# Four-layer decoder on one Trainium2 core: new instruction orders in the second self attention, the last cross attention and the last feed forward

## The chip, the cores and the metric

The kernel runs on one core of one Trainium2 chip. A core has TensorE (PE in the profile: matmuls and transposes, results in PSUM), VectorE (DVE), ScalarE (ACT), GpSimd (POOL) and the DMA queues, here issued by SyncE (SP). Each engine runs its own instruction list in order; they meet only at semaphores. The metric is the device time of one execution in microseconds, as the median of several runs.

## The reference, cut to what matters

The model is a pre-norm decoder of 4 layers over x of 32 × 128 × 128, float32: each layer adds a self attention, a cross attention to a context of 32 × 120 × 96, and a feed forward. Twelve blocks in all. The change touches three of them.

```python
# layer 1, self attention: 16 heads of 8; two inner gradient steps of a small linear model per head
Z = k @ W0;  y1, vjp1 = vjp(ln, Z);  dz1 = vjp1(y1 - v)
KK = tril(k @ k.T);  Z2 = Z - KK @ dz1;  y2, vjp2 = vjp(ln, Z2);  dz2 = vjp2(y2 - v)
ctx = q @ W0 - tril(q @ k.T) @ (dz1 + dz2)
ctx = (ctx - mean) * rsqrt(var + EPS)          # over positions and channels of a head
x = x + (ctx * gn_g + gn_b) @ Wout + bout

# layer 3, cross attention: 16 heads of 8
q = x_hat @ q_w + q_b;  k, v = split(cond @ kv_w + kv_b)
x = x + softmax(q * 8**-0.5 @ k.T) @ v @ proj_w + proj_b

# layer 3, feed forward: product keys, 4 heads, 64 + 64 keys, 8 x 8 candidates, best 8 of 512 experts
sx, sy = top_k(q @ keys, 8);  s, pk = top_k(sx[:, None] + sy[None], 8)
w = silu((x_hat @ down_embed[idx]) * softmax(s))
x = x + silu(x_hat @ W_up.T) @ W_down.T + sum(w * up_embed[idx])
```

## The kernel before, in words

Each block is one function, and the twelve run one after the other. x stays in SBUF for the whole kernel, with 128 positions on the partitions. Inside a block every engine walks the same software pipeline, `skewed(engine, depth, n, per)` (line 180): step t works on item t in role 0, on item t-1 in role 1, and so on to the block's depth. `for b, u in item(2)` reads "the item that is two steps old"; b is its number, u the buffer it uses. The first steps are written out, the rest is a loop with `per` steps in its body. In what order an engine takes the roles' pieces inside one step is written by hand, and this order is what the change is about. `after(engine, semaphore, count)` is a wait that is left out where the count isn't positive; `chain(...)` makes DVE wait for its own instruction before.

*Self attention of layer 1* (`l1_attn`, line 1046): 16 steps' worth of pairs of sequences, depth 3. Role 0: ACT normalises x into x̂ (1209), PE transposes it (1284), ACT copies the transpose (1214), PE projects it with bias products (`projected`, 1252 to 1257) into the two PSUM halves r of `p_s`, ACT copies the projections (1217, 1218 and 1227, 1228) and squares z (1230); DVE reduces the squares (1173), and `gradient` (1126) makes dz1 and the outer products `outer1` (1199). Role 1: PE's `states` (1246) multiplies them by the triangular matrix into `p_s`, DVE's `applied` (1139) reads it (1143, 1146), z2, its squares (1221, 1167), a second gradient and `outer2` (1188). Role 2: the same with `outer2`, then the mean over the sequence by a product with ones (1280), centring (1163, 1164), squares (1224, 1170). Role 3: scaling of the context (1152, 1153), its transposes (1294), ACT's copy (1233), output product (1300), the residual (1177) and the statistics for the next block. The two PSUM halves of `p_s` are shared by `states1`, `states2` and the projections, with DVE's or ACT's reading between each two.

*Cross attention of layer 3* (`l3_xattn`, line 2683): 32 items, depth 4. Role 1: transpose of x̂ (2808), k, v and q products (2829, 2831, 2832). k is spread by head over `kTm` (2752). Role 2: scores with queries on the partitions (2793), four matmuls on four groups of 32 rows into four PSUM banks `p_s`; DVE takes the maximum per head (2730), PE transposes it (2811) and computes the scores transposed (2815) into the same banks, adds the negated maxima (2819), and ACT takes the exponential over all four banks (2773). Role 3: product with the values (2800), ACT's copy (2767), transposes (2825), division by the sum (2746, 2747), transpose of the heads (2835), copy (2781). Role 4: output product (2804), residual (2741), statistics.

*Feed forward of layer 3* (`l3_ffn`, line 2844): 16 pairs, depth 3. Role 0: x̂, transposes (3034), q product (3040), key products (3054). Role 1: DVE picks the best keys of each half and the candidates (2890 to 2905), forms all sums (2913, two instructions of 2048 columns), and ACT takes their exponentials (`exps`, 2950 to 2952). Role 2: dot products (2996), dense up product (3026) with ACT's Silu into hT (2965), masks and weights on DVE (2919 to 2931), ACT's `silus` of r=0. Role 3: `silus` of r=1 (2942, 2943: a Silu and a small one with accumulation for each of 4 heads), DVE adds the rest (`added`, 2878 to 2882), PE sums and transposes the weights over heads (`heads`, 2998 to 3004), ACT's `turned` copies them (2946 to 2948), PE makes the dense and the chosen output (3009, 3011, 3016), ACT copies it to x (2990). A table load (1.28 us) stands before the first exponential and before the first Silu of a step.

## Time and profile before

| | |
|---|---|
| median of 3 runs | 4558.21 us (4552.51 to 4561.47) |
| profiled execution | 4545.59 us |
| its span, first to last instruction | 4543.5 us |
| PE, DVE, ACT, POOL busy | 75%, 62%, 40%, 15% of the span |
| mean granted TensorE clock | 0.817 |

The profile is of one execution. Its busy shares are means over twelve blocks with different limits, so they say little about a block; the rows below are taken from stretches inside the three edited blocks. In a row of a timeline, the first number is the start in microseconds from the span's start and the second the duration; a bracket at the end gives the idle time of the engine before the instruction and who ended it. In a table of windows the last but two numbers are the granted clock of TensorE as a share of 2.4 GHz.

### The profile page before, as it was taken

What the parts mean: (1) busy time and instruction counts of PE and PEld (TensorE: products, weight loads), DVE (VectorE), ACT (ScalarE), POOL (GpSimd) and SP (SyncE); (2) the same over time, 40 slices, a digit from 0 to 9 for tenths busy, and PEclk for the clock granted to TensorE, in tenths of its full rate; (3) what the DMA queues carried; (4) which work ended last, traced back from release to release, by engine and by line L of the source; (5) the groups of instructions that cost most, each with busy time, mean ns of one, the idle gap of its engine ahead of it and who ended that gap; (6) DMA issues with size and microseconds to landing.
All of it is one profiled execution on the core that took longest, in us unless ns stands there. A gap on an engine that the chain in (4) does not pass through costs nothing. (4 is left out here: it accounts for less than half of the span.)

```text
span 4543.5 us, 71024 instructions
## 1 busy us (share of the span) xinstructions
PE 3398.5 (75%) x22014; PEld 2441.9 (54%) x22015; DVE 2817.2 (62%) x8303; ACT 1806.9 (40%) x5212; POOL 678.4 (15%) x867
## 2 busy tenths in 40 slices
PE   3567289456654885765888868999889997876887
PEld 3445289122222563544556755666567775555776
DVE  6556622588785775265886443444457775657886
ACT  1446233111112663212775333222145553436776
POOL 0044523000001776201000110000000000000000
PEclk9789599566766665577777777999989999997888
DMA  4030176100004000523000000000000000000000
GB/s 112 1 160 0 40 235 196 47 0 0 0 0 149 3 0 1 149 65 81 7 0 0 1 10 1 9 9 9 0 19 0 0 0 4 0 0 15 1 0 19
DMA packets 111454, 152.52 MB, mean 34 GB/s; under 512 B 21594, under 2 KB 88216, under 8 KB 109718
## 3 DMA queue, kind: packets, MB, share of 16 engines
q1 hardware_dynamic: 99822, 142.12, 10.1%
q0 software_dynamic: 11520, 9.05, 0.7%
q8 instruction: 52, 0.85, 0.1%
q14 instruction: 60, 0.49, 0.0%
HBM read 107.45 MB, written 58.50 MB: 37 GB/s over the span
## 5 line engine op out<-in xcount | busy, mean ns | idle before, releaser
L1249 PE MATMUL l_attn_p_s<-l_attn_outer,l_attn_upper 128*128 128x512 f32 x256 | 181.9, 876 | 204.4 <-DVE l_attn_outer L1188 131.0
L95 POOL TENSOR_TENSOR rstd<-vareps,minus_half 128x32 f32<-128x32 f32 x11 | 59.8, 5439 | 1456.6 <-DVE vareps L86 1323.6
L398 ACT ACTIVATE l_ffn_sg<-l_ffn_p_g 112x512 f32<-112x512 f32 x192 | 114.7, 597 | 391.9 <-PE l_ffn_p_g L378 367.1
L409 DVE TENSOR_TENSOR l_ffn_h<-l_ffn_sg,l_ffn_p_u 112x512 f32<-112x512 f32 x192 | 131.9, 688 | 172.7 <-PE l_ffn_p_u L381 171.7
L1249 PEld LDWEIGHTS l_attn_p_s<-l_attn_outer,l_attn_upper 128*128 128x128 f32 x256 | 70.2, 288 | 305.2 <-issue 185.5
L381 PE MATMUL l_ffn_p_u<-l_ffn_f_xTall,l_ffn_wu 128*112 x384 | 198.8, 600 | 7.7 <-DVE l_ffn_h L409 7.7
L1408 POOL DMA_INDIRECT slots_in<-l_xattn_x,l_xattn_slot x192 | 190.0, 990 | 82.3 <-issue 50.1
L378 PE MATMUL l_ffn_p_g<-l_ffn_f_xTall,l_ffn_wg 128*112 x384 | 199.0, 600 | 0.9 <-DVE l_ffn_al L2440 0.9
L387 PEld LDWEIGHTS l_ffn_p_o<-l_ffn_wd,l_ffn_h 112*128 112x128 f32 x1536 | 176.6, 192 | 15.7 <-issue 15.7
L2604 ACT ACTIVATE l_attn_E<-l_attn_p_s,l_attn_nm 128x128 f32<-128x128 f32 x512 | 181.2, 386 | 2.8 <-DVE l_attn_nm L2562 2.7
L387 PE MATMUL l_ffn_p_o<-l_ffn_wd,l_ffn_h 112*128 112x128 f32 x1536 | 176.7, 275 | 0.0
L418 DVE SCALAR_TENSOR_TENSOR x<-l_ffn_p_o,l_ffn_cw,x 128x128 f32 x256 | 85.5, 351 | 112.6 <-PE l_ffn_p_o L387 112.6
L2621 PEld LDWEIGHTS l_attn_p_y<-l_attn_xT,l_attn_wqkv 128*128 128x128 f32 x1024 | 131.6, 194 | 34.1 <-issue 32.9
L2621 PE MATMUL l_attn_p_y<-l_attn_xT,l_attn_wqkv 128*128 128x128 f32 x1024 | 137.6, 278 | 1.5 <-DVE l_attn_qT L2566 1.5
L3004 PEld LDWEIGHTS l_ffn_p_w<-ident,l_ffn_w 128*128 128x128 f32 x1024 | 129.8, 207 | 9.4 <-DVE l_ffn_w L2882 5.2
L3004 PE MATMUL l_ffn_p_w<-ident,l_ffn_w 128*128 128x128 f32 x1024 | 130.3, 290 | 5.9 <-DVE l_ffn_w L2882 4.2
L381 PEld LDWEIGHTS l_ffn_p_u<-l_ffn_f_xTall,l_ffn_wu 128*112 128x112 f32 x384 | 68.7, 179 | 106.7 <-issue 98.2
L2604 ACT ACTIVATION_READ_ACCUMULATOR l_attn_E<-l_attn_p_s,l_attn_nm 128x1 f32 x512 | 115.6, 226 | 0.0
L378 PEld LDWEIGHTS l_ffn_p_g<-l_ffn_f_xTall,l_ffn_wg 128*112 128x112 f32 x384 | 66.6, 179 | 83.4 <-issue 82.8
L3040 PE MATMUL l_ffn_p_q<-l_ffn_xT,l_ffn_wq 128*128 128x256 f32 x128 | 55.6, 609 | 59.3 <-ACT l_ffn_xT L2968 59.3
L2562 DVE TENSOR_REDUCE l_attn_nm<-l_attn_p_s 128x8 f32<-128x1024 f32 x64 | 78.1, 1221 | 30.6 <-PE l_attn_p_s L2648 30.6
L2773 ACT ACTIVATE l_xattn_E<-l_xattn_p_s 120x2048 f32<-120x2048 f32 x32 | 60.1, 1878 | 91.3 <-PE l_xattn_p_s L2819 91.3
(785 smaller groups left out, 9545.8 us busy)
## 6 DMA issues: line engine op xcount, KB each, us to landing
l_experts_w<-in_L_ffn_w SPq DMA_DIRECT2D x72, 512.0 KB, 4.2
slots_in<-l_xattn_empty SPq DMA_DIRECT2D x8, 2145.0 KB, 24.0
shares_out<-l_xattn_zero SPq DMA_DIRECT2D x24, 512.0 KB, 11.3
l_combine_got<-shares_out SPq DMA_DIRECT2D x16, 768.0 KB, 4.4
l_attn_toep<-kernel_rows SPq DMA_DIRECT2D x1, 8192.0 KB, 31.8
xattn_toep<-ssm_rows SPq DMA_DIRECT2D x1, 8192.0 KB
l_slots_w<-in_L_ffn_w SPq DMA_DIRECT2D x32, 176.0 KB, 2.3
l_experts_x<-slots_in SPq DMA_DIRECT2D x72, 65.0 KB
```

The lines of the kernel that those rows point to most:

```text
L378: pe.matmul(X.p_g[0:X.FP, k % 2], X.wg[:, w, f * X.FP:(f + 1) * X.FP], x, start=True, stop=True).then_inc(s.gate_psum, 1)
L381: pe.matmul(X.p_u[0:X.FP, k % 2], X.wu[:, w, f * X.FP:(f + 1) * X.FP], x, start=True, stop=True).then_inc(s.up_psum, 1)
L387: mm = pe.matmul(X.p_o[:, v, q * P:(q + 1) * P], X.h[:, v, f, q * P:(q + 1) * P], X.wd[:, w, f * P:(f + 1) * P], start=(f == 0), stop=(f = ...
L398: act.activation(X.sg[:, k % 2], X.p_g[0:X.FP, k % 2], ACT.Silu).then_inc(s.silu_ready, 1)
L409: dve.tensor_tensor(X.h[:, k // X.FC, k % X.FC], X.sg[:, k % 2], X.p_u[0:X.FP, k % 2], ALU.mult).then_inc(s.h_ready, 1)
L418: add = dve.scalar_tensor_tensor(out=row(R.x, b), in0=X.p_o[:, v, q * P:(q + 1) * P], scalar=weight, in1=row(R.x, b), op0=ALU.mult, op1=AL ...
L1249: mm = pe.matmul(p_s[:, r, a], upper[:], outer[:, r, a * 512:(a + 1) * 512], start=True, stop=True)
L1408: pool.indirect_dma_start(xb, bass.IndirectOffsetOnAxis(ap=slot[:, b, k:k + 1], axis=0), x6[:, u, k], None, bounds_check=last, oob_is_err= ...
L2562: dve.tensor_reduce(nm[:, u % 2], p_s[:, u % 2].rearrange("p a (h t) -> p (a h) t", t=P), AX.X, ALU.max, negate=True).then_inc(s.max_ready, 1)
L2604: e = act.activation(E[:, u % 2, h], p_s[:, u % 2, odd, c * P:(c + 1) * P], ACT.Exp, bias=nm[:, u % 2, h:h + 1], accum_out=sums[:, u % 2, ...
L2621: mm = pe.matmul(p_y[:, c * P:(c + 1) * P], wqkv[:, w:w + P], xT[:, u // 2], start=True, stop=True)
L3004: mm = pe.matmul(p_w[:, c * P:(c + 1) * P], w[:, v, r, n:n + P], R.ident[:], start=(h == 0), stop=(h == H - 1))
```

## The change

Only orders inside a step change, with the semaphore counts that go with them, and three pieces are split in two. No arithmetic, buffer or DMA is added or removed.

- Self attention: PE transposes x̂ and the context before `states1` and projects both halves behind the mean. ACT copies the context's transpose right after that of x̂, then both halves of the projections and their square, and only then the squares of roles 1 and 2. DVE adds the residual and takes the statistics before the three reductions of squares.
- Cross attention: scores, maxima and the exponential go in halves of two banks, and the first half of the scores waits for the first half of the exponential only. q and the copy of v stand before the exponential on ACT. PE transposes x̂ and the heads right behind the scores (the heads a step later than before), makes v and q before the transposition of the maxima, and the output product and k before the shift. DVE takes the rows and heads last.
- Feed forward: ACT's Silus of r=1 are split in two pairs of heads with hT and xT between them; both `exps` come before `turned(1)`; DVE's second `added` comes behind the sums.

```diff
 # l1_attn, DVE (moved up, now before the three reductions of squares)
+                    for b, u in item(3):  # wait xb_ready, out_psum; x = xb + p_o; pair_stats
 ...
 # l1_attn, ACT
-                    for b, u in item(0):
                         act.wait_ge(s.xT_psum, b + 1)
                         act.activation(xT[:], p_t[:, 0:W], ACT.Copy).then_inc(s.xT_ready, 1)
+                    for b, u in item(3):
+                        act.wait_ge(s.ctxT_psum, b + 1)
+                        act.activation(cT[:], p_c[:, 0:W], ACT.Copy).then_inc(s.ctxT_ready, 1)
+                    for b, u in item(0):
+                        for r in range(2):
+                            act.wait_ge(s.proj_psum, b * 2 + (r + 1))
+                            # the two copies into proj[:, u, :, r], then_inc(s.proj_read, 1)
+                        act.wait_ge(s.proj_read, b * 2 + 2)
+                        act.activation(t1[:], z[u], ACT.Square).then_inc(s.sq1_ready, 1)
                     # then Square of z2 (item 1), Square of qw (item 2)
 ...
 # l1_attn, PE, after states2 of item(2)
+                    for b, u in item(0):  # wait xhat_ready; two transposes into p_t; xT_psum
+                    for b, u in item(3):  # wait ctx_ready; two transposes into p_c; ctxT_psum
                     for b, u in item(1):  # states1
                     for b, u in item(2):  # mean
                     for b, u in item(0):
                         pe.wait_ge(s.xT_ready, b + 1)
                         projected(b, 0)
                         projected(b, 1)
                     for b, u in item(3):  # output product
 # l3_xattn, POOL
-                        after(pool, s.vq_psum, b - 1)
+                        after(pool, s.kT_psum, b - 1)
 # l3_xattn, DVE
-                        dve.wait_ge(s.scores_psum, b + 1)
-                        dve.tensor_reduce(nm[...][:, :, 0:SUB], p_s[:, :, 0:SUB * SC]...).then_inc(s.max_ready, 1)
+                        for r in range(2):
+                            dve.wait_ge(s.scores_psum, b * 2 + (r + 1))
+                            last = dve.tensor_reduce(nm[...][:, 2 * r:2 * r + 2, 0:SUB], p_s[:, 2 * r:2 * r + 2, 0:SUB * SC]...)
+                        last.then_inc(s.max_ready, 1)
 # DVE's order: max(2), xhat(0), nmB(2), x(4), kTm(1), statistics(4), rows and heads(3)
 # l3_xattn, ACT's order: wait xT_psum(1), wait headsT_psum(4), xT(1), headsT(4), oT(3), qT and va(1), then
+                    for b, u in item(2):
+                        act.wait_ge(s.shifted_psum, b + 1)
+                        for r in range(2):
+                            act.activation(E[0:SC, 2 * r:2 * r + 2], p_s[0:SC, 2 * r:2 * r + 2], ACT.Exp).then_inc(s.exp_ready, 1)
 # l3_xattn, PE
-                        after(pe, s.exp_ready, b)
                         for j in range(4):
+                            if j % 2 == 0:
+                                after(pe, s.exp_ready, b * 2 - 1 + j // 2)
                             mm = pe.matmul(p_s[:, j, 0:SUB * SC], qT[rows, u % 2], kTm[...], start=True, stop=True)
-                        mm.then_inc(s.scores_psum, 1)
+                            if j % 2:
+                                mm.then_inc(s.scores_psum, 1)
 # PE's order: scores(2), transpose of xhat(1), of heads(4), values(3), v and q(1), transposition of
 # the maxima and transposed scores(2), output(4), wait shift_spread, k(1), shift(2), rows(3)
 # l3_ffn, DVE
                     for b, v in item(3):
                         added(b, v, 0)
-                        added(b, v, 1)
                     for b, v in item(1):  # sums, two instructions
+                    for b, v in item(3):
+                        added(b, v, 1)
 # l3_ffn, ACT
                     for b, v in item(3):
-                        silus(b, v, 1)
+                        silus(b, v, 1, (0, 1))
                     for b, v in item(2):  # hT
                     for b, v in item(0):  # xT
+                    for b, v in item(3):
+                        silus(b, v, 1, (2, 3)).then_inc(s.silu_ready, 1)
+                    for b, v in item(0):  # qT
 ...
                     for b, v in item(1):
                         exps(b, v, 0)
+                    for b, v in item(1):
+                        exps(b, v, 1).then_inc(s.exp_ready, 1)
                     for b, v in item(3):
                         turned(b, 1)
-                    for b, v in item(1):
-                        exps(b, v, 1).then_inc(s.exp_ready, 1)
```

## Rows read from the trace of the kernel before

**Rows 1.** Windows: stretch, us, busy us (instructions) by engine, granted clock, DMA share, GB/s
```profile
840.00:1420.00 580.00, 327.84 (x704) 144.38 (x704) 456.65 (x830) 78.04 (x223) 13.07 (x17) 0.69 0.00 1
...
3900.00:4060.00 160.00, 129.73 (x1902) 81.85 (x1901) 97.47 (x188) 65.66 (x122) 14.47 (x42) 1.00 0.00 0
...
4143.66:4165.90 22.24, 18.50 (x128) 16.88 (x128) 21.93 (x50) 14.84 (x24) 0.00 (x0) 0.85 0.00 1
...
4321.09:4347.39 26.30, 21.21 (x136) 18.75 (x135) 22.02 (x51) 18.57 (x38) 0.00 (x0) 0.87 0.00 0
4165.90:4478.10 312.20, 250.79 (x1642) 221.81 (x1642) 264.27 (x590) 226.66 (x456) 0.00 (x0) 0.89 0.00 0
...
4332.20:4335.80 3.60, 3.57 (x8) 2.87 (x9) 3.56 (x4) 0.00 (x0) 0.00 (x0) 0.50 0.00 0
```

**Rows 2.** DVE's waits in the self attention: who for whom, us, times, longest
```profile
DVE l_attn_st L1173 <- ACT l_attn_t L1230: 44.6, 15, 3.9
```

**Rows 3.** Timeline of the self attention, one pair: start, duration, instruction, wait before
```profile
1137.24 0.30 PE L1280 MATMUL l_attn_p_m<-l_attn_gs,ones 128*128 128x32 f32 x2
...
1138.35 0.91 PE L1256 MATMUL l_attn_p_s<-l_attn_wproj,l_attn_xT 128*128 128x384 f32 x2 [0.56 <-ACT l_attn_xT L1214]
...
1145.01 0.69 PE L1294 MATMUL l_attn_p_c<-ident,l_attn_proj 128*128 128x128 f32 x2
...
1146.65 1.23 PE L1300 MATMUL l_attn_p_o<-l_attn_wout,l_attn_cT 128*128 128x128 f32 x4 [0.95 <-ACT l_attn_cT L1233]
...
1148.10 0.42 DVE L1177 TENSOR_TENSOR x<-l_attn_xb,l_attn_p_o 128x256 f32 x1 [1.32 <-PE l_attn_p_o L1300]
...
1149.86 0.35 DVE L1128 RECIPROCAL l_attn_st<-l_attn_st 128x32 f32<-128x32 f32 x1
...
1164.86 0.42 DVE L1153 TENSOR_TENSOR l_attn_proj<-l_attn_proj,l_attn_st 128x256 f32<-128x256 f32 x1
...
1166.47 5.40 PE L1249 MATMUL l_attn_p_s<-l_attn_outer,l_attn_upper 128*128 128x512 f32 x8 [4.46 <-DVE l_attn_part L1143]
```

**Rows 4.** The cross attention's exponential: durations ns, first and last start
```profile
L2773 ACT ACTIVATE l_xattn_E<-l_xattn_p_s x32: 1877/1878/1879, 3835.1 to 4081.9; 120x2048 f32<-120x2048 f32 x32
```

**Rows 5.** Timeline of the cross attention, one item; the first row ends with four records
```profile
3948.94 0.69 PE L2793 MATMUL l_xattn_p_s<-l_xattn_kTm,l_xattn_qT 32*128 32x480 f32 x4 [0.71 <-ACT l_xattn_qT L2778]
...
3949.95 1.08 PE L2800 MATMUL l_xattn_p_av<-l_xattn_E,l_xattn_va 120*32 120x128 f32 x32
3950.08 2.16 DVE L2730 TENSOR_REDUCE l_xattn_nm<-l_xattn_p_s 128x16 f32<-128x1920 f32 x1 [1.26 <-PE l_xattn_p_s L2793]
...
3953.53 1.04 PE L2819 MATMUL l_xattn_p_s<-l_xattn_nmB,ones 32*120 32x512 f32 x8
...
3954.63 1.88 ACT L2773 ACTIVATE l_xattn_E<-l_xattn_p_s 120x2048 f32<-120x2048 f32 x1 [2.75 <-PE l_xattn_p_s L2819]
...
3956.40 0.36 ACT L2778 ACTIVATE l_xattn_qT<-l_xattn_p_a,l_xattn_bq 128x128 f32<-128x128 f32 x1
...
3956.86 1.09 PE L2793 MATMUL l_xattn_p_s<-l_xattn_kTm,l_xattn_qT 32*128 32x480 f32 x8 [0.64 <-ACT l_xattn_qT L2778]
```

**Rows 6.** Timeline of the feed forward, one pair
```profile
4327.13 0.71 ACT L2942 ACTIVATE l_ffn_w<-l_ffn_w,l_ffn_rz 128x512 f32<-128x512 f32 x1
...
4330.90 1.00 ACT L2965 ACTIVATE l_ffn_hT<-l_ffn_p_q 128x1024 f32<-128x1024 f32 x1
4331.03 0.17 DVE L2882 TENSOR_TENSOR l_ffn_w<-l_ffn_w,l_ffn_rest 128x4 f32<-128x4 f32 x1 [3.88 <-ACT l_ffn_e_c L2943]
4331.11 4.48 DVE L2913 TENSOR_TENSOR l_ffn_sums<-l_ffn_xs,l_ffn_p_sim 128x2048 f32<-128x2048 f32 x2
...
4332.23 3.78 PE L3040 MATMUL l_ffn_p_q<-l_ffn_xT,l_ffn_wq 128*128 128x256 f32 x8 [4.51 <-ACT l_ffn_xT L2968]
...
4345.37 0.60 ACT L2948 ACTIVATE l_ffn_wT<-l_ffn_p_w 128x512 f32<-128x512 f32 x1 [2.29 <-PE l_ffn_p_w L3004]
4345.87 1.91 ACT L2952 ACTIVATE l_ffn_w<-l_ffn_sums 128x2048 f32<-128x2048 f32 x1
```

More of the change, by code:

```diff
@@ L1173, in _ @@
                         dve.tensor_reduce(st1[:, 0], heads(t1[:]), AX.X, ALU.add).then_inc(s.var1_ready, 1)
-                    for b, u in item(3):
-                        dve.wait_ge(s.xb_ready, b + 1)
-                        dve.wait_ge(s.out_psum, b + 1)
-                        dve.tensor_tensor(pair(R.x, b), side(xb[:]), side(p_o[:, 0:W]), ALU.add).then_inc(s.out_taken, 1)
-                        dve.wait_ge(s.out_taken, b + 1)
-                        chain(dve.tensor_copy(means[:, 0:1], eps[:]))
-                        chain(pair_stats(R, dve, b, chain))
                     for b, u in item(1):
@@ L2758, in _ @@
                             dve.tensor_copy(R.stats[:, bass.ds(b - (PER - 1), PER), :], R.aggr[:, 0:PER])
+                    for b, u in item(3):
+                        dve.wait_ge(s.rows_psum, b + 1)
+                        av = p_r[:].rearrange("p m (j e) -> p m j e", j=4)
+                        chain(dve.reciprocal(rden[:].rearrange("p (m j) -> p m j", m=SUB), av[:, :, :, HD]))
+                        dve.tensor_tensor(heads[:].rearrange("p (j m e) -> p m j e", m=SUB, j=4), av[:, :, :, 0:HD],
+                                          rden[:].rearrange("p (m j) -> p m j", m=SUB).unsqueeze(3).broadcast_to((P, SUB, 4, HD)),
+                                          ALU.mult).then_inc(s.heads_ready, 1)
             @block.scalar
@@ L2764, in _ @@
                 for item in skewed(act, 4):
+                    for b, u in item(1):
+                        act.wait_ge(s.xT_psum, b + 1)
+                    for b, u in item(4):
+                        act.wait_ge(s.headsT_psum, b + 1)
+                    for b, u in item(1):
+                        act.activation(xT[:], p_a[:, 0:P], ACT.Copy).then_inc(s.xT_ready, 1)
+                    for b, u in item(4):
+                        act.activation(headsT[:], p_a[:, 384:512], ACT.Copy).then_inc(s.headsT_ready, 1)
                     for b, u in item(3):
@@ L2768, in _ @@
                     for b, u in item(1):
-                        act.wait_ge(s.xT_psum, b + 1)
-                        act.activation(xT[:], p_a[:, 0:P], ACT.Copy).then_inc(s.xT_ready, 1)
-                    for b, u in item(2):
-                        act.wait_ge(s.shifted_psum, b + 1)
-                        act.activation(E[0:SC], p_s[0:SC], ACT.Exp).then_inc(s.exp_ready, 1)
-                    for b, u in item(3):
-                        act.wait_ge(s.headsT_psum, b + 1)
-                    for b, u in item(1):
                         act.wait_ge(s.vq_psum, b + 1)
@@ L2779, in _ @@
                         act.activation(va[0:SC, u, :, 0:HD], p_a[0:SC, P:256].rearrange("p (h e) -> p h e", h=H), ACT.Copy).then_inc(s.va_ready, 1)
-                    for b, u in item(3):
-                        act.activation(headsT[:], p_a[:, 384:512], ACT.Copy).then_inc(s.headsT_ready, 1)
+                    for b, u in item(2):
+                        act.wait_ge(s.shifted_psum, b + 1)
+                        for r in range(2):
+                            act.activation(E[0:SC, 2 * r:2 * r + 2], p_s[0:SC, 2 * r:2 * r + 2], ACT.Exp).then_inc(s.exp_ready, 1)
             @block.tensor
@@ L2815, in _ @@
                                 pe.matmul(p_s[0:SC, j, m * P:(m + 1) * P], kTm[rows, u % 2, m], qT[rows, u % 2], start=(m == 0), stop=False)
+                    for b, u in item(4):
+                        pe.matmul(p_r[:, 0], headsT[:], wo[:], start=True, stop=True).then_inc(s.out_psum, 1)
+                    for b, u in item(2):
                         pe.wait_ge(s.shift_spread, b + 1)
+                    for b, u in item(1):
+                        pe.matmul(p_c[:, 0:SC], wkv[:, 0:P], cT[:, u % 2], start=True, stop=True).then_inc(s.kT_psum, 1)
+                    for b, u in item(2):
                         for j in range(4):
@@ L2936, in _, with silus @@
             def _(act):
-                def silus(b, v, r):
+                def silus(b, v, r, heads):
                     u = v % PER2
                     act.wait_ge(s.w_ready, b * 2 + (r + 1))
-                    for h in range(H):
+                    for h in heads:
                         n, g = slice(h * NE, (h + 1) * NE), r * H + h
```

79 lines of the change are left out of this document (31 added, 48 removed).

## The prediction

> **What bounds the kernel now.** The page comes first: no engine is busy for more than three quarters of the span, so the bound has to be looked for stage by stage. The second view is the table of windows [rows 1]: the reader is to see that DVE (VectorE) is the busiest engine in two of the edited stages, 457 of 580 us in the self attention and 264 of 312 in the feed forward's loop, and PE (TensorE) in the cross attention, 130 of 160. Then come the waits, and last the timeline of one period of each loop.
>
> Self attention (16 pairs): DVE's longest wait is for the squares of the newest item, 44.6 us over 15 pairs [rows 2]; a second one, 1.32 us, is for the output product [rows 3]. Both wait for PE's work after the products of `states`: mean (1137.24), transposes of x̂, a trip to ACT (ScalarE) and back, the projections (1138.35 to 1145.01), transposes of the context, another trip to ACT, the output product (1146.65) [rows 3].
>
> Cross attention (32 items): the exponentials run from 3835.1 to 4081.9, 31 intervals, 7.96 us each [rows 4]. The timeline shows one ring: scores 3948.94, maximum 3950.08, its transposition and the transposed scores, shift 3953.53, exponential 3954.63, the copy of q that stands behind it on ACT 3956.40, the next scores 3956.86 [rows 5].
>
> Feed forward (16 pairs): DVE waits 3.88 us a pair for the last Silus [rows 6]. One period without that wait is in the trace, 22.24 us, against 26.30 with it, and twelve periods from 4165.90 on take 312.2 us [rows 1]. DVE is the victim. The ring that sets 26.3 runs through ACT and PE: xT copied, q product, two head transpositions, turned(1), exps(1), table load, Silus of r=0, output copy, x̂, Silus of r=1, hT, xT again.
>
> **The change part by part.**
>
> *Self attention.* The x̂ and context transposes move ahead of `states1`, into PE's 4.46 us of waiting before 1166.47 [rows 3]. The context is scaled at 1165.3 (1164.86 plus 0.42) and its two transposes take 0.69 at the slow clock, so 0.4 us of cover is left; if it were gone, a pair would pay the overrun. Behind `states1` then stand the mean, 0.25 us, and the projections, which today come 1.11 after the mean's start: 0.85 us earlier. The output product follows them at once, its operand copied long before. Today the projections end at 1145.01 and DVE begins the next gradient at 1149.86. In the new order they end at 1144.15, the output product reaches DVE 1.4 later (1146.65 to 1148.10 today), DVE has 1.75 us of residual and statistics (1148.10 to 1149.86) and then three reductions that I take at 0.4 each, 1.2: gradient at 1148.5, 1.4 us saved. The two Squares that now queue on ACT behind the second projection copy are ready some 2.1 us after the projections, before DVE wants them at 3.2 after, so they cost nothing where item 3 exists; in the two filling steps without it they eat the gain. What is late next is the output product, with 3.5 us of DVE's waiting. Thirteen steps hold items 0 and 3: 13 × 1.4 = 18 us, between 0.7 a step (the transposes delay `states1`; 9 us) and 2.3 (the slow part of the projections becomes fast; 30 us).
>
> *Cross attention.* Put the exponential's start at 0. A 1024-column activation takes 1.00 us [rows 6], and ACT starts the next 0.11 before the end (3954.63 + 1.88 against 3956.40 [rows 5]): the halves end at 1.00 and 1.9. PE reacts 0.10 later (3956.40 + 0.36 against 3956.86): first scores at 1.10, second at 2.0. What a pair of these products costs no row shows. All four, on four groups of rows, take 1.01 us to the next product (3948.94 to 3949.95): a pair takes at least half, 0.50, and at most 1.01. The first four of the eight records last 0.69 and all eight 1.09 [rows 5], two passes side by side, so I take 0.85, near the upper end.
> Then, in PE's new order: two transposes, which I take at 0.2 (3.1), attention times values, 1.0 (4.1), v and q, 0.4 (4.5). Beside it DVE: first scores done at 2.2, two maxima of 1.12 (half of 2.16, plus 0.04), done at 4.45. The two strands meet at 4.5. From there to the shift it is 1.25 today (maximum's end 3952.24 to 3953.53), now with the output product and kT in between, 0.2 each, and 1.10 from the shift to the exponential: 7.3 us. Against 7.96 that is 0.65; times 30 it is 19 us. A pair at 0.50 leaves the maxima last (7.2), at 1.01 it gives 7.45; with 0.1 for reactions, 12 to 24 us. The later rows and heads are hidden: DVE has them some 1.2 after the exponential starts, PE wants them at 2.9. POOL's copy of the context waits for one product more and feeds two items later; it costs nothing. No DMA is moved anywhere.
> The page "TensorE: Matmul & The Clock Gate" of the Trainium skill (section "Part 3: Packing small matmuls — row/col tiling") says that matmuls on distinct row groups run side by side in about the time of one. By that a pair costs as much as four, the split puts a second full stretch on PE, and the period would be 7.45, not 7.3. The eight records agree with the side-by-side running; no row has a pair alone.
>
> *Feed forward.* hT and xT stand behind two of the four Silus of r=1 now, and the other two run on ACT while PE makes q: four take 3.77 us (4327.13 to 4330.90), so xT is ready 1.88 earlier. exps(1), 1.91 us, stands behind turned(1) today (4345.87), for which ACT has waited 2.29 us; put ahead of it, it fits into that wait [rows 6]. The ring loses 1.88 + 1.91: 26.3 − 3.8 = 22.5 us. On DVE the large sums (4.48 us) move ahead of the second addition, which then comes after the Silus and stops waiting; DVE's own period is 22.24. The later of the two is 22.5: 312.2 − 12 × 22.5 = 42 us, and of the wait in the one further step that has sums to hide it some 2: together 44. In the last two steps there are no sums and the waits stay. Bounds: 48 (22.24 throughout) and 22 (the ring loses only the first 1.88). What is late next: q on ACT, behind the other two Silus, by under 0.1 us.
>
> Sum: 18 + 19 + 44 = 81 us. The profiled execution took 4545.6 us around its span of 4543.5; less 81 it is 4464.6. It is 12.6 below the median of 4558.2, so the median comes to 4477.
>
> **The rivals.**
> *Warmer clock, more gain.* q takes 3.78 us after 4.51 of PE's idling, all of it at a granted clock of 0.50, that is 1.2 GHz [rows 1, 6]. Shorter idle stretches may leave PE at 2.4 GHz in all three rings. Then self attention gives 30, cross attention 24, feed forward, capped by DVE, 48: 102 us, 4456. Against it: in the self attention PE's idling before `outer2`, where the clock falls, is not shortened by any edit.
> The same page (section "HAM oscillation — how this bites in real kernels") says that waits between bursts bring the clock down; the rows on q agree, and by it the feed forward's ring is the one to gain, which DVE then caps.
> *Rings only half cut.* If exps(1) ahead of turned(1) delays the second turn as much as it saves, only 1.88 a period goes (22 us and 1 for the last step); if each half of maximum, scores and exponential pays a full start, the cross attention gives 8; with 12 from the self attention it is 43, 4515. For it: in the feed forward DVE and the ring nearly tie, and coupled loops lose at both. Against it: the 2.29 us that ACT has free.
> *Slower: the cross attention's clock falls.* It is granted 1.00 there today with PE busy 130 of 160 us [rows 1]. The change makes a wait of 0.8 us for the first half of the exponential. At 1.2 GHz the matmuls, some 5 us of issue an item, take twice that: 5 us an item, up to 150. That gives 4558 − 62 + 150 = 4646, and it decides from 13 slow items on (62 / 5). Against it: PE waits 0.64 us once an item for q today and at full clock [rows 5], and the fall in the feed forward follows 4.51.
> *It doesn't do what it says:* a wait that I did not see holds each ring where it is; 4558. The period of 22.24 and the free 4.46 us speak against it.
>
> **How the numbers follow.** Forecast 0.57 (4477, its own range 4464 to 4496), half cut 0.18, warmer 0.18, no change 0.04, slower 0.03. About 0.2%, 9 us, is what a measurement here can tell from no change: faster 0.93, same 0.04, slower 0.03. The range 4454 to 4510 takes in most of the warmer case and the fast side of the half-cut one; about 2 in 10 stay out.
>
> **What would show it.** Right: in the self attention a wait of DVE near 3.5 us for the output product, none for the squares, and pairs 1.4 us closer together; exponentials in twos, every 7.3 us; in the feed forward no wait at the second addition and a period of 22.3 to 22.6. Wrong: `states1` starting later than its bank is free; the transposition of the maxima beyond 4.6 us after the exponential's start; turned(1) or q late by over 1 us; a granted clock under 0.95 in the cross attention.

## The result, and the profile after

The change makes the kernel faster, by a little less than forecast. In 4 runs each on the same chip the median is 4486.25 us (4482.76 to 4487.40) against 4556.92 before: a ratio of 0.9844, 95% interval 0.9827 to 0.9861, or 70.7 us where 81 were forecast. The total hides a miss, which the stages show. They are cut at the single instruction in which DVE prepares the next stage's normalization; the profiled executions took 4545.59 and 4482.76 us, one of each kernel.

| stage, us | before | after | difference | forecast |
|---|---|---|---|---|
| second self attention | 592.1 | 567.2 | −24.9 | −18 |
| unedited stretch behind it | 2396.6 | 2401.2 | +4.6 | 0 |
| last cross attention | 277.2 | 282.2 | **+5.0** | −19 |
| last feed forward | 451.4 | 402.8 | −48.6 | −44 |
| span | 4543.5 | 4480.9 | −62.6 | −81 |

Not every stage is equally still. With identical code the self attention took 564.1 to 575.4 us in the ten profiled kernels that hold the changed version (mean 569.8), and the unedited stretch 2396.6 to 2408.2 in all of them; the changed cross attention took 282.2 in six kernels and 283.4 in a seventh, the changed feed forward 401.3 to 404.3. So 5 us are much in the last two stages and little in the first two. Of the kernel before there is one profiled execution; how far its 592.1 us scatter is not known.

The first view is the table of windows of the kernel after; columns as in [rows 1]. The lines are the self attention, the stretch behind it, the cross attention and the feed forward, then one period of the feed forward, then the stretch that [rows 1] shows of the cross attention.

```profile
827.52:1394.72 567.20, 327.30 (x714) 145.65 (x714) 456.23 (x834) 82.45 (x225) 17.05 (x17) 0.70 0.01 3
1394.72:3795.91 2401.19, 1995.72 (x11051) 1424.74 (x11114) 1419.66 (x4797) 1015.18 (x3454) 372.29 (x364) 0.81 0.08 24
3795.91:4078.08 282.17, 246.19 (x3040) 144.21 (x3040) 165.48 (x334) 112.75 (x224) 28.93 (x65) 0.95 0.01 2
4078.08:4480.90 402.82, 327.33 (x2208) 285.70 (x2208) 351.61 (x786) 305.83 (x607) 5.45 (x1) 0.92 0.03 10
...
4306.39:4328.70 22.31, 19.32 (x141) 16.89 (x139) 21.91 (x50) 19.19 (x39) 0.00 (x0) 1.00 0.00 0
3900.00:4060.00 160.00, 148.92 (x1898) 87.37 (x1899) 101.19 (x204) 69.71 (x141) 14.24 (x38) 1.00 0.00 0
```

In the cross attention PE is busy 148.9 of 160 us, where it was 129.7 [rows 1], at a granted clock of 1.00 both times. The products are the same and so is the clock. The rows of the scores account for most of it: in pairs all eight records take 1.99 us where they took 1.09 [rows 5], 0.9 in each of 20 items. Not all of it lengthens the item, since the first pair runs beside the second half of the exponential. In the feed forward this period takes 22.31 us and DVE is busy for 21.91 of them, with the clock at 1.00 where it was 0.87 in the period of [rows 1]; over 4180 to 4400 us it is 0.96, where it was 0.90.

The timeline of the self attention, one pair (start, duration, instruction, wait before), answers to [rows 3]:

```profile
1150.35 0.44 PE L1277 MATMUL l_attn_p_c<-ident,l_attn_proj 128*128 128x128 f32 x2 [3.31 <-DVE l_attn_proj L1153]
1151.48 5.40 PE L1245 MATMUL l_attn_p_s<-l_attn_outer,l_attn_upper 128*128 128x512 f32 x8 [0.69 <-DVE l_attn_part L1143]
1156.72 0.30 PE L1286 MATMUL l_attn_p_m<-l_attn_gs,ones 128*128 128x32 f32 x2
1156.98 0.91 PE L1252 MATMUL l_attn_p_s<-l_attn_wproj,l_attn_xT 128*128 128x384 f32 x2
...
1162.84 0.71 PE L1295 MATMUL l_attn_p_o<-l_attn_wout,l_attn_cT 128*128 128x128 f32 x4
```

```profile
1163.77 0.42 DVE L1168 TENSOR_TENSOR x<-l_attn_xb,l_attn_p_o 128x256 f32 x1 [2.29 <-PE l_attn_p_o L1295]
...
1166.52 0.34 DVE L1128 RECIPROCAL l_attn_st<-l_attn_st 128x32 f32<-128x32 f32 x1
```

The projections start 0.26 us behind the mean and not 1.11. The context's transposes lie in PE's wait, and `states1` still starts as soon as DVE has released its bank. DVE begins the gradient 3.7 us after the projections' end (1162.84 to 1166.52), before 4.85. Over all pairs with a residual it is 3.7 to 4.2, before 4.3 to 5.0. Its waits in the whole stage (who for whom, us, times, longest), before and then after:

```profile
DVE l_attn_st L1173 <- ACT l_attn_t L1230: 58.1, 16, 13.5
DVE x L1177 <- PE l_attn_p_o L1300: 20.7, 16, 2.5
```

```profile
DVE x L1168 <- PE l_attn_p_o L1295: 41.1, 15, 5.5
DVE l_attn_st L1180 <- ACT l_attn_t L1223: 13.5, 1, 13.5
```

The 13.5 us are one wait at the first filling step, the same in both kernels; [rows 2] leaves it out. Of the 44.6 us for the other squares 6.5 are left, in two filling steps; the wait for the output product has doubled in their place.

The timeline of the cross attention, PE and then ACT and DVE, one item, answers to [rows 5]. PEld is PE's loading of weights; the row shown is that of the second pair of scores:

```profile
3948.60 1.99 PE L2793 MATMUL l_xattn_p_s<-l_xattn_kTm,l_xattn_qT 32*128 32x480 f32 x8 [0.56 <-ACT l_xattn_E L2780]
3949.51 0.30 PEld L2793 LDWEIGHTS l_xattn_p_s<-l_xattn_kTm,l_xattn_qT 32*128 32x128 f32 x4 [0.62 <-ACT l_xattn_E L2780]
...
3950.52 0.33 PE L2799 MATMUL l_xattn_p_a<-ident,l_xattn_xhat 128*128 128x128 f32 x1
3950.68 0.27 PE L2802 MATMUL l_xattn_p_a<-ident,l_xattn_heads 128*128 128x128 f32 x1
3950.88 1.08 PE L2808 MATMUL l_xattn_p_av<-l_xattn_E,l_xattn_va 120*32 120x128 f32 x32
3951.89 0.48 PE L2815 MATMUL l_xattn_p_a<-l_xattn_wkv,l_xattn_cT 97*120 97x128 f32 x2
...
3952.43 0.27 PE L2819 MATMUL l_xattn_p_c<-ident,l_xattn_nm 128*128 128x128 f32 x1
3952.64 1.15 PE L2823 MATMUL l_xattn_p_s<-l_xattn_qT,l_xattn_kTm 32*120 32x128 f32 x32
3953.72 0.49 PE L2825 MATMUL l_xattn_p_r<-l_xattn_wo,l_xattn_headsT 128*128 128x128 f32 x2
3954.04 0.38 PE L2829 MATMUL l_xattn_p_c<-l_xattn_cT,l_xattn_wkv 97*128 97x120 f32 x2
3954.35 1.14 PE L2833 MATMUL l_xattn_p_s<-l_xattn_nmB,ones 32*120 32x512 f32 x8
```

```profile
3947.52 1.94 ACT L2780 ACTIVATE l_xattn_E<-l_xattn_p_s 120x1024 f32<-120x1024 f32 x2 [2.38 <-PE l_xattn_p_s L2833]
3949.72 2.22 DVE L2726 TENSOR_REDUCE l_xattn_nm<-l_xattn_p_s 128x8 f32<-128x960 f32 x2 [0.99 <-PE l_xattn_p_s L2793]
```

The next exponential starts at 3955.55: 8.03 us an item, where 7.96 were measured [rows 4] and 7.3 forecast. The maxima end 4.42 us after the exponential's start (3951.94), as forecast, but nobody waits for them: PE reaches their transposition at 3952.43, straight from other products. The ring, the closed chain of work and waits that sets the period, is this: both halves of the exponential on ACT (the second pair of scores starts at 3949.51, released by the second half), then PE's list from that pair to the shift without a wait, then the next exponential.

The timeline of the feed forward, PE's q and ACT's part of the ring, answers to [rows 6]:

```profile
4309.72 1.99 PE L3049 MATMUL l_ffn_p_q<-l_ffn_xT,l_ffn_wq 128*128 128x256 f32 x8 [1.81 <-ACT l_ffn_xT L2974]
```

```profile
4316.37 0.60 ACT L2954 ACTIVATE l_ffn_wT<-l_ffn_p_w 128x512 f32<-128x512 f32 x1 [1.51 <-PE l_ffn_p_w L3013]
4316.87 3.71 ACT L2958 ACTIVATE l_ffn_w<-l_ffn_sums 128x2048 f32<-128x2048 f32 x2
4321.06 0.60 ACT L2954 ACTIVATE l_ffn_wT<-l_ffn_p_w 128x512 f32<-128x512 f32 x1 [0.49 <-PE l_ffn_p_w L3013]
```

Both exponentials stand behind turned(0), and turned(1) still waits 0.49 us for PE: it lost nothing. q takes 1.99 us where it took 3.78 at half the clock [rows 6].

### The profile page after: what moved, and what is told of

The parts are those of the page before. It is cut to its first block and busy times, and to the rows that moved or that the text cites. A ratio compares the mean times of both kernels' runs of the same rounds, so it can differ in the third digit from the quotient of the medians.

```text
span 4480.9 us, 71181 instructions
## 1 busy us (share of the span) xinstructions
PE 3408.7 (76%) x21951; PEld 2441.9 (54%) x22015; DVE 2820.6 (63%) x8335; ACT 1822.0 (41%) x5244; POOL 680.2 (15%) x867
## 5 line engine op out<-in xcount | busy, mean ns | idle before, releaser
L3013 PEld LDWEIGHTS l_ffn_p_w<-ident,l_ffn_w 128*128 128x128 f32 x1024 | 125.1, 202 | 22.3 <-DVE l_ffn_w L2887 21.5
L2948 ACT ACTIVATE l_ffn_w<-l_ffn_w,l_ffn_rz 128x512 f32<-128x512 f32 x128 | 91.1, 712 | 13.6 <-DVE l_ffn_w L2937 13.4
L2233 PE MATMUL l_film_p_m<-l_film_diag,l_film_e 128*120 128x256 f32 x256 | 91.8, 524 | 4.6 <-issue 4.6
```

The source lines that it names most:

```text
L2233: mm = pe.matmul(p_m[0:SC, 0:256], e[:, u % 2, h], diag[:, h].rearrange("p k t -> p (k t)"), start=(h == 0), stop=(h == H - 1))
L2948: act.activation(w[:, v, r, n], w[:, v, r, n], ACT.Silu, scale=rz[:, u, g:g + 1])
L3013: mm = pe.matmul(p_w[:, c * P:(c + 1) * P], w[:, v, r, n:n + P], R.ident[:], start=(h == 0), stop=(h == H - 1))
```

## The experiments

**Is it the new cross attention itself, or a disturbance from elsewhere?** The first kernel is the changed one with the cross attention's function of before, whole.

> The changed kernel with the cross attention of before put back; self attention and feed forward stay changed. Theory (the new cross attention is itself slower: its stage, between the two starts of the norm, takes 282.2 us against 277.2): the stage comes back to 277 with a period of 7.96 us, and the whole is 5 us below the changed kernel, 4481. Rival (the difference between the stages is scatter between executions): the stage stays within 1 us of 282, whole 4486.

It took 4479.59 us (4475.39 to 4484.03, 4 runs), 0.9843 of before (0.9827 to 0.986), and its cross attention 277.2 us, as before, for 282.2. The loss is the new cross attention's own. The whole-kernel intervals could not have told that; the stage does.

**Why is PE's list longer?** The scores, the transposed scores and the shift run on groups of 32 rows; the transposes and the other products use 97, 120 or all 128 rows (full-row products below). The change sets the output product and k between the transposed scores and the shift. The second kernel takes the cross attention of before and moves only the output product there:

```diff
@@ PE, cross attention of before
-   output product (before the transposition of the maxima)
    transposed scores
+   output product
    shift
```

> The cross attention of before, with one edit: the output product (two records) stands between the transposed scores and the shift, that is, full-row work between two pieces on 32-row groups, on the ring. Theory A (PE pays for each change between 32-row groups and full rows): in the changed kernel two products there took 0.73 us where their own issue is 0.42, and the shift took 0.1 more to reach the exponential; one product costs 0.4 to 0.5, period 8.35 to 8.45. Theory B (changes are free, a product costs its 0.21): period 8.17.

The stage took 296.0 us for 277.2: 0.59 us for each of 32 items, by a product that was there anyway. Most items take 8.55 us, where most took 7.93; that is above the 8.35 to 8.45 that I expected, so the direction held and the size was too small. The execution took 4490.91. PE's timeline in it:

```profile
3935.43 1.15 PE L2809 MATMUL l_xattn_p_s<-l_xattn_qT,l_xattn_kTm 32*120 32x128 f32 x32
3936.51 0.49 PE L2811 MATMUL l_xattn_p_r<-l_xattn_wo,l_xattn_headsT 128*128 128x128 f32 x2
3936.93 1.13 PE L2816 MATMUL l_xattn_p_s<-l_xattn_nmB,ones 32*120 32x512 f32 x8
```

The 0.62 us between 7.93 and 8.55 can be read off by subtracting starts. The product itself is 0.22 of it (the third kernel, below, shows it beside full-row products): before, it lay where PE waited for the maxima, now it is in the ring. The other 0.40 is the price of two borders between kinds of work: the transposed scores hold PE for 1.08 us (3935.43 to 3936.51) and not 0.98 (3952.55 to 3953.53 [rows 5]), the output product for 0.42 and not 0.22, and the shift reaches the exponential in 1.20 and not 1.10.

The third kernel is the changed one with the opposite edit:

```diff
@@ PE, changed cross attention
    v, q
+   k, output product
    transposition of the maxima
    transposed scores
-   output product, k
    shift
```

> The changed kernel with k's and the output product moved on PE from between transposed scores and shift to right behind v and q, so that transposed scores and shift stand together. The same products, the same number of them on the ring. Theory A (changes between 32-row groups and full rows cost PE time): the 0.3 of the extra and 0.1 at the exponential go, period 8.03 to between 7.6 and 7.75. Theory B (only the amount of work counts): period stays 8.03.

The stage took 267.8 us, 14.4 less than the change's, 7.63 us an item for 8.03 (in all 4468.02). PE's timeline in it:

```profile
3950.15 0.38 PE L2817 MATMUL l_xattn_p_c<-l_xattn_cT,l_xattn_wkv 97*128 97x120 f32 x2
3950.37 0.39 PE L2819 MATMUL l_xattn_p_r<-l_xattn_wo,l_xattn_headsT 128*128 128x128 f32 x2
3950.60 0.27 PE L2822 MATMUL l_xattn_p_c<-ident,l_xattn_nm 128*128 128x128 f32 x1
3950.80 1.15 PE L2826 MATMUL l_xattn_p_s<-l_xattn_qT,l_xattn_kTm 32*120 32x128 f32 x32
3951.77 1.04 PE L2831 MATMUL l_xattn_p_s<-l_xattn_nmB,ones 32*120 32x512 f32 x8
```

Subtracting starts, the 0.40 us splits in three. The transposed scores hold PE for 0.97 us when the shift follows and for 1.08 when a full-row product does. The output product and k cost 0.45 beside other full-row products (3950.15 to 3950.60) and 0.63 between the two (3953.72 to 3954.35), about 0.1 on each of them. From the shift's start to the exponential it is 1.10 when row groups stand before it (exponential at 3952.87) and 1.20 when it comes from a full-row product. So PE pays when it goes from one kind to the other: four times 0.1 us for two borders, about 0.2 us a border, in this kernel and in the one before it. The loading of the weights shows it too. Beside its own kind a product's weights are loaded 0.11 us ahead of it; behind a border they are not:

```profile
3951.66 0.31 PEld L2831 LDWEIGHTS l_xattn_p_s<-l_xattn_nmB,ones 32*120 32x120 f32 x8
```

```profile
3954.35 0.30 PEld L2833 LDWEIGHTS l_xattn_p_s<-l_xattn_nmB,ones 32*120 32x120 f32 x8
```

The first is the shift of this kernel, whose product starts at 3951.77; the second is that of the changed kernel, whose product starts at 3954.35 as well. The page "TensorEngine Tiling (Array Packing)" of the Trainium skill, section "Key Properties", says that changing the tiling mode drains TensorE. These rows agree with it.

**What are the halves worth?** The fourth kernel is the changed one with scores, maxima and exponential undivided, in the new order.

```diff
@@ changed cross attention, ACT (PE and DVE in the same way)
-   for r in range(2): exponential of banks 2r, 2r+1
+   exponential of all four banks
```

> The changed kernel's new order in the cross attention, but scores, maxima and exponential whole as before. My account of the ring: a pair of score products costs PE as much as all four (1.0 us), so PE is done with the scores 3.0 us after the exponential's start either way; only the maxima come later (5.4 instead of 4.4), and the transposition of the maxima then waits 0.5: period 8.5. Rival (halving brings nothing at all, since PE is the bound anyway): 8.0. Second rival (halves cost PE a second start): under 8.0, as PE gets a microsecond back.

The stage took 298.0 us, 8.5 an item as expected (in all 4506.93). So the halves gain 15.8 us in the new order, and the order alone costs 20.8 on the cross attention of before. In its rows the two products between transposed scores and shift cost 0.83 us an item (0.73 to the shift, 0.10 behind it), and 0.21 come back since q's copy no longer stands between the exponential and the scores. The change's 5.0 is the difference of two large terms.

**Can the rest of PE's list be shortened?** The fifth kernel puts the k product and the transpose of x̂ into the gap in which PE waits for the first half of the exponential:

```diff
@@ PE, against the third kernel; DVE masks the keys first, takes the statistics last
+   k, transpose of x̂
    scores, two pairs
-   transpose of x̂
    transpose of the heads, attention times values
    v, q, output product          (k no longer here)
    transposition of the maxima, transposed scores, shift
```

> The changed kernel with its last cross attention rearranged once more: TensorE does the key transpose and the transpose of the normalized rows in the gap before the first pair of score products, then the four score products, the transposes of the masked exponentials, the value product, v, q and the output product in one uninterrupted stretch of full-row products, and then the transposed scores with nothing between them and the shift; VectorE masks the keys first and takes the statistics last. Theory A (each change between products in groups of 32 rows and full-row products costs TensorE 0.1 to 0.3 us, and its list is the ring): the two transposes (0.36 us at the least) move into a gap of 0.56 us in which TensorE waits for the exponentials, so the item goes below the 7.63 us that it has with the output product behind v and q: 7.3 to 7.5 us, a stage of 257 to 262 us where that one has 267.8 and the change 282.2, in all about 4460 us. Theory B (only the one product between transposed scores and shift mattered, and the rest of the list is hidden): 7.6 us, 267 to 268 us. Theory C (the masking of the keys, now first on VectorE, delays the maxima): over 7.8 us.

The stage took 258.7 us, in all 4461.52; 24 of the 31 periods are at or under 7.31 us. PE in it, the start of an item:

```profile
3907.51 0.38 PE L2789 MATMUL l_xattn_p_c<-l_xattn_cT,l_xattn_wkv 97*128 97x120 f32 x2
3907.73 0.28 PE L2792 MATMUL l_xattn_p_a<-ident,l_xattn_xhat 128*128 128x128 f32 x1
3908.23 1.99 PE L2800 MATMUL l_xattn_p_s<-l_xattn_kTm,l_xattn_qT 32*128 32x480 f32 x8 [0.23 <-ACT l_xattn_E L2780]
```

The idle 0.56 us has become 0.23, and the period fell from the third kernel's 7.63 by the 0.32 that left the list behind the scores. That PE's list is in the ring is shown twice over. Seven periods take 7.63 to 7.65: there DVE has copied the statistics of four items, masks the keys later, and PE waits 0.1 us for the maxima. What theory C names happens in these items, at 7.63 us and not at its 7.8.

**Self attention: which edit carries the gain?** One kernel keeps the changed PE order and ACT's early copy of the context, and puts back the squares (between the two projection copies) and DVE's residual (behind the reductions):

> The changed kernel, in whose second self attention ScalarE does the squares between the two copies of the projections again and VectorE the residual after the three gradient reductions, as before; TensorE's new order and ScalarE's early context copy stay. Theory A (the ring runs over the mean, the projections, the gradient and the updated weight, and nothing of it waits for the output product once TensorE makes that early; VectorE's residual and the undivided copies of the projections only lengthen it): the gradient is done 2.7 us after the projections' end and not 3.5, 0.75 us a pair by 13 pairs, some 10 us: the self attention stage 555 to 560 us where the change has 567.2 (564.2 to 575.4 in the runs so far), in all 4470 to 4478. Theory B (the move of the residual on VectorE carries the gain, since it frees the residual's buffers and the following normalization): the stage goes back towards 592, above 580, in all above 4495.

The other keeps of the change only the residual's new place on DVE:

> The changed kernel with the second self attention of before, of whose change only one part is kept: VectorE adds the residual before the three gradient reductions. Theory A: the residual waits for the output product, which TensorE makes late here, so that wait goes into the ring: the gradient comes about 1.2 us a pair later than before, and the stage takes 600 to 612 us where before it took 592.1, in all 4515 to 4525. Theory B (VectorE's order carries the gain): the stage is at 565 to 580, in all about 4485.

The first took 559.2 us, as expected and under all ten runs of the changed stage, but 4482.66 us in all, above the 4470 to 4478: stretches that it does not edit were longer. The second took 604.9, above before's 592.1, and 4526.42 in all. The changed kernel owes its gain to the rest of the new order, not to the move of the residual: alone that costs 13 us. This is little more than the stage's scatter, but the pairs say the same without the scatter. From the projections' end to the gradient they take 4.3 to 5.0 us before, 5.3 to 6.0 with the move alone, 3.7 to 4.2 in the change and 3.3 to 3.4 in attn_keep (the 13 pairs with a residual). DVE's waits in the two, in the order in which they are told:

```profile
DVE l_attn_st L1173 <- ACT l_attn_t L1232: 49.8, 16, 13.5
```

```profile
DVE x L1168 <- PE l_attn_p_o L1300: 75.6, 16, 6.4
```

In attn_keep DVE waits 49.8 us for squares and once, 2.5 us, for the output product, together 52.3; the change waits 61.1 for both (41.1, 13.5 and 6.5). The 9 us between them are about the 8 us of the stage. In attn_dve the 75.6 us for the output product, 20.7 before, replace most of the wait for squares: both together are 95.3 for 86.4. My account of the size was too large: I expected 0.75 us a pair between projections' end and gradient, and the means of the 13 pairs are 3.4 and 3.9. attn_keep puts back two edits at once. How much of the gain is the residual's and how much that of the squares, in the new order, is not separated.

**Feed forward: do the parts add?** Four parts of the changed stage were undone in four kernels: the early exponentials; the split Silus; both of these; the order of the additions on DVE.

```diff
@@ ACT, feed forward: ffn_turned, and ffn_both
-   exps(1), turned(1)
+   turned(1), exps(1)
@@ ACT, feed forward: ffn_silus, and ffn_both
-   Silus 0 and 1, hT, xT, Silus 2 and 3
+   Silus 0 to 3, hT, xT
@@ DVE, feed forward: ffn_added
-   sums, added(1)
+   added(1), sums
```

> The changed kernel, in whose last feed forward ScalarE does the second exponentials behind the second turned copies again, as before; the Silus stay split. Account by rings: the exponentials, 1.9 us, stand again in the ring from the turned copies over the products to the Silus, which goes from 22.5 to 24.4 us a pair, above VectorE's 22.3; by 12 to 16 pairs the stage takes 425 to 436 us where the change has 402.8, in all 4505 to 4518. Rival: VectorE's list hides it, 403 to 408 us, and then the split of the Silus alone carried the gain.

> The changed kernel, in whose last feed forward the second row's four Silus stand together ahead of the copies for hT and xT again, as before; the exponentials stay early. Account by rings: 1.88 us come back into the ring over xT, q, the candidates and the Silus. With the exponentials back alone the pair measured 23.7 us for 22.33, so the ring without either is 21.8 and not the 22.5 of my sum; here it should again be 23.5 to 24.0, the stage 415 to 423 us where the change has 402.8, in all 4492 to 4505. Rival (the early exponentials carried nearly all): 403 to 408 us.

> The changed kernel, in whose last feed forward both the exponentials are late and the Silus are undivided again, as before; only the order of the additions on VectorE stays new. If the two parts lie in one ring, they add: 21.8 + 1.9 + 1.9 = 25.6 us a pair or, with TensorE at the lower clock for the q products again (3.78 us for 1.99), 26 to 27.5; the stage 440 to 455 us (before 451.4), in all 4520 to 4535. Rival (they lie in different rings, and each alone decides): 415 to 425 us.

> The changed kernel, in whose last feed forward VectorE does the second row's addition behind its first half of sums again, ahead of the row's maxima, as before; the Silus stay split. Since the last two Silus are now later than the copies, VectorE would wait for them: 1 to 2 us a pair on the engine that is the bound, period 23.3 to 24.3, the stage 415 to 432 us where the change has 402.8, in all 4492 to 4515. Rival (the Silus are done before VectorE gets there, and the move is worth nothing): 402 to 404 us.

| kernel | stage, us | above the change | one period | in all |
|---|---|---|---|---|
| ffn_turned | 416.6 | 13.8 | 23.7 in the longer ones | 4494.11 |
| ffn_silus | 415.8 | 13.0 | 23.8 in most | 4508.19 |
| ffn_both | 450.1 | 47.3 | 25.4 to 26.8 | 4542.63 |
| ffn_added | 402.8 | 0.0 | 22.33 | 4492.26 |

All experiments but the first and the last are one execution each, on chips where the kernel before takes 4550.7 to 4559.0, so their stages and periods are compared and not their totals. The expected totals of ffn_silus and ffn_both were too low by 3 and 8 us; their self attention, which no edit touches, took 575.0 and 573.1.

Each part alone costs 13 to 14 us when undone, both together 47, so they lie in one ring and DVE cuts off what is under 22.3. The first miss was of size: I expected 22 to 34 for the exponentials. By my estimate a ring of 23.7 with one part of 1.9 undone has 21.8 with none, 0.5 under DVE's period; DVE hides it, so no run shows the 21.8 itself. The windows of one period each, ffn_silus and ffn_both:

```profile
4279.20:4302.96 23.76, 20.25 (x140) 18.47 (x139) 22.02 (x49) 19.03 (x39) 0.00 (x0) 0.93 0.00 0
```

```profile
4317.38:4344.16 26.78, 21.68 (x140) 19.22 (x139) 22.11 (x49) 19.03 (x39) 0.00 (x0) 0.87 0.00 0
```

With both undone the long periods average 26.1 us, a little more than 21.8 + 3.8. The clock fits this: in these periods it is granted at 0.93 of full speed with one part undone and at 0.87 with both, as before the change, and over the stretch from 4180 to 4400 at 0.90 in ffn_both and 0.96 in the change. Before and in ffn_both q follows 4.5 us of PE's idling and takes 3.4 to 3.8 us in all steady pairs. In the change, behind 1.7 to 1.9 us, it takes 1.99 in half of the steady pairs and 2.4 to 3.6 in the others, so the lower level is rarer but not gone; the period is 22.3 either way. What the clock is worth apart from the two edits, no run separates.

The order of the additions is worth nothing here: with it undone DVE had no wait in the loop. My account of that part was wrong, and so was the expectation.

**A better version.** The last kernel joins the changed feed forward, the self attention of attn_keep and the cross attention of x_fill.

> Three parts together: the changed feed forward; the self attention with the squares between the copies and VectorE's residual behind the reductions (559.2 us in its one run, 567.2 in the change); the cross attention with the key and row transposes in the gap before the first score products and the output product with v and q (258.7 us for 282.2). Their sum from the change's 4486.25: less 23.5 and 8 to 10, that is 4453 to 4456, with 4448 to 4462 for the scatter of the stretches that no edit touches; against before 0.977 to 0.979. If the gain of the self attention was scatter of its clock, 4460 to 4465.

Five runs gave 4459.84 us (4455.03 to 4464.68), 0.9789 of before (0.9775 to 0.9803, before's median 4559.01 on that chip). The change's interval begins at 0.9827, so this version is faster than both kernels, than the change by about 0.55%. The forecast of 4453 to 4456 was missed by 4 us, inside the 4448 to 4462 given for scatter, and the time lies at the edge of the rival's 4460 to 4465. The stages of its profiled execution: 562.8, 2402.2, 258.6, 402.7. The self attention came out between the two levels, again under all ten runs of the changed one, by 1.3 us; its pairs take 3.4 us from the projections' end to the gradient, as in attn_keep. So its gain is seen in the pairs; its size in the stage, 7 and 11 us against the mean of ten, rests on two executions.

## Why the prediction was right, and where it failed

The forecast of 4477 was 9 us too low, in its own range, by errors of both signs that partly cancel.

- **Self attention, −18 forecast.** The mechanism held: projections 0.85 us earlier in the pair shown, the squares' wait gone but for filling steps, the output product late next, `states1` not delayed. 25 us by the one execution, 22 by the mean of ten against before's one, in the forecast's bounds of 9 to 30. I took 13 pairs of 1.4; 22 by 13 is 1.7. The rows of the 13 pairs give the same: the projections start 0.33 us behind the mean's start and not 1.11, and the gradient begins 3.9 after their end and not 4.7. The term that I had too small is the second. I let the output product reach DVE 1.4 later, from a row at a granted clock of 0.50 (1145 to 1150 us); in the new order it takes 0.93 in pairs such as the one shown (1162.84 to 1163.77), with the products before it at 1.00, and 1.45 in others (1130.67 to 1132.12). So part of the extra is clock, and that part was luck. I did not see that one of the edits which I priced inside the sum, the residual ahead of the reductions, is a loss.
- **Cross attention, −19 forecast: the step that failed.** "The halves end at 1.00 and 1.9" and "done at 4.45" held to 0.05 us. What failed is PE's list, and my own sign of it came: the transposition of the maxima stands 4.91 us after the exponential's start, beyond 4.6. From that start: the second pair holds PE for 1.01 and not 0.85; the two transposes cost 0.36 and not 0.2; v and q 0.54 and not 0.4; from there to the shift 1.92 (from 3952.43) and not 1.65; shift to exponential 1.20 and not 1.10. Together some 0.8, which is the gap from 7.25 to 8.03. The rule on the row groups from the page of the Trainium skill that I weighed and set aside for 0.85 ("TensorE: Matmul & The Clock Gate", section "Part 3: Packing small matmuls — row/col tiling") was right: two groups take as long as four (1.01 between the scores and the next product in [rows 5]). By it the sum would have been 7.45, still 0.6 short. The larger part was in no term: I priced each product by its row in the old neighbourhood, and the change moved products across the border between full-row and row-group work. The third kernel shows 0.40 of it. The rest, some 0.3 at the transposes and at v, was not undone by itself; that these are borders too (PE's work on either side has another shape) is argued, not shown. The "half cut" rival (8 us gained) was nearer here, but still had the sign wrong. Of its reason, a full start for each half, the part on the scores held; dividing the maximum and dividing the exponential cost 0.06 us each. The clock did not fall (1.00 in both stretches); that rival is out.
- **Feed forward, −44 forecast, 48.6 measured.** Both parts of 1.9 us were in the ring as said, and turned(1) did not suffer. The ring was sized 22.5, where by my estimate from the experiments it is 21.8. q takes its 1.99 us at full clock in half of the steady pairs of the change and in none before: the rival "warmer clock" was right in part in this stage, and DVE caps it, as it said. The 48.6 stand at its bound of 48. DVE's period, 22.24 in the forecast, is 22.33. The third edit, the additions, I counted as DVE's release from its wait; the ring's shortening had done that already.

The stages sum to −68.5 and the rest to +5.9, which is within the scatter of stretches that nothing edits. The medians say −70.7.

## What to carry to other kernels

- When TensorE's list is near the bound, price an order by its borders as well as by its products: count how often it changes between products on row groups and on full rows, and keep each kind together. A product of 0.22 us cost 0.59 more in the wrong place than in the right one: its own time, which had been hidden, and 0.4 for two borders.
- A ring that is 3.8 us too long is worth fixing only down to the next engine's period. Size the ring with the durations at the clock that the repaired loop will have, and take each part's worth from undoing it alone and together.
- An edit that helps the engine in front (residual early) may put a late operand into the ring. Undo each edit once: one cost 13 us when it was made alone, and one was worth nothing.

## What the runs showed of the hardware

- Two score products on two row groups hold TensorE 1.01 us (3949.51 to 3950.52), as long as four on four (3948.94 to 3949.95 [rows 5]).
- A change between full-row products and row-group products costs it about 0.2 us, at a granted clock of 1.00: 0.1 on the last work before the border and 0.1 on the first behind it (the transposed scores 1.08 for 0.97, the shift 1.20 to the exponential for 1.10). Behind a border the weights are not loaded 0.11 us ahead, as they are within a stretch (3954.35 for 3954.35; 3951.66 for 3951.77).
- The exponential of 2048 columns takes 1.88 us and in two halves 1.94, so halving cost ACT 0.06; halving the maximum cost DVE 0.06 (2.22 for 2.16).
- The same self attention code scattered by 11 us between executions, with the granted clock of the whole at 0.815 to 0.824 and that of the stage at 0.69 to 0.71. In the change's profiled execution the steady pairs take between 31.5 and 35.6 us. A gain of 8 us there needs several executions, or the rows of single pairs, to be seen.
